# Splitting the last two down panels of every tile into two sweeps over output blocks

## The reference, cut to what matters

```python
gate = lora_add(jnp.einsum('bnh,fh->bnf', x, W_gate), x, A_gate, B_gate)
up   = lora_add(jnp.einsum('bnh,fh->bnf', x, W_up), x, A_up, B_up)
act  = jax.nn.silu(gate) * up
down = lora_add(jnp.einsum('bnf,hf->bnh', act, W_down), act, A_down, B_down)
return x + down
```

## Time and profile before

| | us |
|---|---|
| median of 3 runs | 2187.39 (2184.78 to 2189.65) |
| profiled execution | 2185.16 |
| its span in the trace | 2183.5 |

### The profile page before, as it was taken

The page is one execution under the profiler, slowest core; times in us unless marked ns, Lnnn a source line. Parts: engine busy times, 40 slices in busy tenths (PEclk is TensorE's granted clock), DMA queues, the critical chain, the costliest instruction groups (busy, mean ns, idle before and its releaser), DMA issues.

```text
span 2183.5 us, 34214 instructions
## 1 busy us (share of the span) xinstructions
PE 2087.3 (96%) x10432; PEld 1774.5 (81%) x10432; DVE 1610.3 (74%) x2144; ACT 971.2 (44%) x1282; POOL 99.0 (5%) x167
## 2 busy tenths in 40 slices
PE   2998999999996899999999999999999999999998
PEld 2997888888885788888888888888888888878887
DVE  7777999999997778787877337458787878753433
ACT  2222888788883533333433325343333333333232
POOL 3110000000001230000000000000000000000000
PEclk9999999999998999999999999999999999999999
DMA  5999999989986664333434995444343434264543
GB/s 194 376 364 347 351 349 356 356 331 349 351 345 235 188 199 129 93 110 89 110 92 147 252 259 187 173 120 118 91 110 94 108 96 108 70 217 159 183 154 125
DMA packets 254658, 441.49 MB, mean 202 GB/s; under 512 B 146902, under 2 KB 147094, under 8 KB 234390
## 3 DMA queue, kind: packets, MB, share of 16 engines
q1 hardware_dynamic: 241046, 408.69, 56.4%
q0 software_dynamic: 11392, 32.01, 4.4%
q10 hardware_dynamic: 2176, 0.26, 0.1%
HBM read 400.74 MB, written 63.73 MB: 213 GB/s over the span
## 4 chain that ended last, share of the span: by engine, by line
PE 82%; DVE 8%; DMA 4%; ACT 2%; issue 2%; DVEq 1%; POOL 0%; ACTq 0%; SPq 0%; POOLq 0%
PE ps L1849 19%; PE ps L1850 19%; PE ps L1851 19%; PE ps L1793 4%; PE ps L1795 4%; PE ps L1794 4%; PE ps L1769 4%; DMA W<-in_w 3%; PE ps L1894 2%; PE ps L1893 2%; DVE wl L1318 2%; PE ps L1802 1%; PE ps L1925 1%; PE ps L1926 1%; DMA araw<-picked_a 1%
## 5 line engine op out<-in xcount | busy, mean ns | idle before, releaser
L1849 PE MATMUL ps<-bh,oph 128*128 128x512 f32 x1216 | 476.3, 392 | 9.2 <-ACT tmp L807 6.0
L1850 PE MATMUL ps<-bl,oph 128*128 128x512 f32 x1216 | 475.8, 391 | 0.0
L1851 PE MATMUL ps<-bh,opl 128*128 128x512 f32 x1216 | 474.2, 390 | 0.0
L1318 DVE TENSOR_TENSOR wl<-W,wh 128x2048 fp32r<-128x2048 f32 x152 | 343.6, 2285 | 9.9 <-ACT wh L742 9.0
L1406 DVE TENSOR_TENSOR tmp<-ps,tmp 128x512 f32<-128x512 f32 (+1 forms) x340 | 234.1, 689 | 132.0 <-PE ps L1894 67.5
L742 ACT ACTIVATE wh<-W 128x2048 fp32r<-128x2048 f32 x152 | 290.7, 1915 | 61.0 <-DMA W<-in_w 55.1
L1403 DVE TENSOR_TENSOR wdl<-wraw,wdh 128x1024 fp32r<-128x1024 f32 x92 | 112.6, 1224 | 264.2 <-ACT wdh L807 264.2
L1849 PE MATMUL ps<-acb_h,wdh 128*128 128x512 f32 (+1 forms) x736 | 280.8, 382 | 4.8 <-DVE acb_l L1403 4.8
L1850 PE MATMUL ps<-acb_l,wdh 128*128 128x512 f32 (+1 forms) x736 | 279.8, 380 | 0.0
L1851 PE MATMUL ps<-acb_h,wdl 128*128 128x512 f32 (+1 forms) x736 | 279.7, 380 | 0.0
L1849 PEld LDWEIGHTS ps<-bh,oph 128*128 128x128 f32 x1216 | 229.4, 189 | 54.6 <-DVE opl L1403 10.4
(11 more groups left out here) (205 smaller groups left out, 2794.9 us busy)
## 6 DMA issues: line engine op xcount, KB each, us to landing
W<-in_w SPq DMA_DIRECT2D x152, 1024.0 KB, 6.9
raw<-in_wgu SPq DMA_DIRECT2D x168, 256.0 KB, 2.7
wraw<-in_wd SPq DMA_DIRECT2D x84, 512.0 KB
toep<-kpad SPq DMA_DIRECT2D x32, 1024.0 KB, 9.3
lraw<-picked_b SPq DMA_DIRECT2D x88, 256.0 KB, 3.8
raw<-kept_acts SPq DMA_DIRECT2D x88, 256.0 KB, 3.4
kept_acts<-tmp SPq DMA_DIRECT2D x84, 256.0 KB, 2.3
picked_b<-in_lora_b POOLq DMA_DIRECT2D x32, 352.0 KB, 4.9
```

The source lines that it names most:

```text
L1318: V.tensor_tensor(out=wl[:, c], in0=W[:, c], in1=wh[:, c].bitcast(F32), op=ALU.subtract).then_inc(w_lo, 1)
L1849: mm(to, lhsT=wh, rhs=mh, start=start, stop=False)
L1850: mm(to, lhsT=wh, rhs=ml, start=False, stop=False)
L1851: return mm(to, lhsT=wl, rhs=mh, start=False, stop=stop)
```

## The change

The loop over pairs of panels is one round shorter. Panel 20 of each tile is written out whole. Panels 21 and 22 are then run in two sweeps: blocks 0 to 3 of panel 21, blocks 0 to 3 of panel 22, blocks 4 to 7 of panel 21, blocks 4 to 7 of panel 22. `panel_done` is raised for panel 21 after its last block, thus at three quarters of the two panels' work, and for panel 22 at the end. Nothing else is edited; ACT, DVE, SP and GpSimd keep their programs.

```diff
+            def last_panels(tile):
+
+                end, a = (tile + 1) * NPAN, (FT - 1) % 2
+                pe.wait_ge(wd_lo, end - 2)
+                pe.wait_ge(ac_lo, (tile + 1) * FT - 2)
+                down(tile, end - 3, a, range(LT)).then_inc(panel_done, 1)
+                for outs in (range(LT // 2), range(LT // 2, LT)):
+                    pe.wait_ge(wd_lo, end - 1)
+                    pe.wait_ge(ac_lo, (tile + 1) * FT - 1)
+                    earlier = down(tile, end - 2, 1 - a, outs)
+                    pe.wait_ge(wd_lo, end)
+                    pe.wait_ge(ac_lo, (tile + 1) * FT)
+                    last = down(tile, end - 1, a, outs, stop=True)
+                    if LT - 1 in outs:
+                        earlier.then_inc(panel_done, 1)
+                        last.then_inc(panel_done, 1)
+
             def other_panels(tile):
...
-                with pe.Fori(0, (NPAN - HALF_AT - 3) // 2) as i:
+                pairs = (NPAN - HALF_AT - 3) // 2
+                with pe.Fori(0, pairs - 1) as i:
                     panel_pair(tile, HALF_AT + 2, i)
-                pe.wait_ge(wd_lo, (tile + 1) * NPAN)
-                pe.wait_ge(ac_lo, (tile + 1) * FT)
-                down(tile, tile * NPAN + NPAN - 1, (FT - 1) % 2, range(LT), stop=True).then_inc(panel_done, 1)
+                last_panels(tile)
```

## The result

The changed kernel took 2195.82 us (median of 8 runs, 2193.18 to 2203.22) against 2186.09 for the kernel before (8 runs beside it, 2183.8 to 2189.65): ratio 1.0041, 95% interval 1.0027 to 1.0055. It is slower by 0.4%, as forecast (2195.0). Its profiled execution took 2194.26, span 2192.6, which is 9.1 us above the span of before; the sum had said 7.6. The two medians lie 9.7 apart, and the interval of the ratio spans 5.9 to 12.0 us, so the timed runs show that there is a loss but don't fix its size; the traces do.

What follows compares the result with a forecast made beforehand. PE, busy 96% of the span, was taken to bound the kernel. Terms 4.88 (starts of tiles 1 and 3) + 2.64 (stage 1) + 0.62 - 0.5 (tile 3) = +7.6 us gave 2195.0, range 2190.5 to 2199.5.

Steps and rivals of the forecast that it cites:

- Gate 1: End of each tile's first sweep: PE waits for panel 22's low parts, wanted after half a panel; 0.62 us per tile.
- Gates 1 to 3: Starts of tiles 1 and 3: waits before panel 22, for the first add, before panel 1; 0.62 + 1.33 + 0.49 = 2.44 us.
- Gate 4: Tile 1 to stage 1: PE waits for an add, 0.92 us, then for `apl`, 1.10; with gate 1, 2.64.
- Tail: End of tile 3: the first store goes out earlier, so the second no longer queues behind it; -0.5 us.
- Sum: Whole kernel, all waits less the gain at the end: +7.6 us, 0.35%.
- Late loads: Rival, tiles 1 and 3: panel 3's loads run beside the stores and come late; +9.6 us, 2197.0; 12%.
- Early adds: Rival, tile ends: adds run early and panel 21's late report costs nothing; +2.0 us, 2189.4; 7%.
- the chain fits: Rival, panel 22's copy: ACT and DVE ready within 2.72 us, so only the store's head start remains; -0.5, 2186.9; 7%.
- The clock rival: New idle gaps halve PE's clock: 5.4 us more per panel, +18 at two starts, 2206; 2%.
- My gaps are at most 1.3: Argument against a clock fall: PE's new idle gaps stay within 1.3 us, while a window with 2 us idle kept full clock.
- gate 2: Starts of tiles 1 and 3: PE waits for DVE's first add, queued behind the late `panel_lo(0)`; 1.33 us with restart.

Runs made afterwards that it cites:

- short_chain: The changed kernel with panel 22's weights copied and subtracted in two halves, so PE's first sweep over it waits for the first half only; ratio 1.0028.
- late_report: The kernel before, whole panels without sweeps, with only panel 21's report moved to the first matmul of block 4 of panel 22; ratio 1.0041.
- dve_order: The changed kernel with adds 0 to 3 put ahead of the next low parts in DVE's order at tile ends; ratio 1.0024.
- control: The kernel before, unchanged, profiled a second time; ratio 1.0001.
- split53: The changed kernel with sweeps of five and three blocks instead of four and four, in all tiles; ratio 1.0032.
- tile3_split53: The kernel before with sweeps of five and three blocks in tile 3 alone, tiles 0 to 2 as before; ratio 1.0003.

## Why the prediction was right

- **Gate 1**, 0.62 a tile: measured 0.70 (tile 3 to the last matmul, 11.09 against 10.39). PE went on 0.15 us after `acb_l`'s end (1306.24 + 0.68 to 1307.07), where the earlier trace rows had 0.06. short_chain shows the mechanism.
- **Gates 1 to 3** at the starts of tiles 1 and 3, 2.44 each: measured 2.67 and 2.61. Late_report and dve_order show the two causes, report and order. By the starts of successive matmuls, 0.227 apart where nothing waits, the three gates at the start of tile 1 took 0.69, 1.41 and 0.43, against 0.62, 1.33 and 0.49 in the sum; the 0.1 that is left over is spread thin and not explained.
- **Gate 4** with gate 1, 2.64: measured 2.63 against control. The memsets came 24.20 us after tile 1's anchor instead of 19.44, thus 4.8 later and not about 3, and stayed hidden: the copy at 1455.50 still waited 7.71 for PE.
- **Tail**, -0.5: measured -0.6, with landings of 5.0 and 5.0. All ten profiles agree: where the second store is issued 2.7 us behind the first (before, control, late_report) they take 5.1 and 5.6, where it is 4.8 to 5.4 behind, 5.0 and 5.0. The estimate of 4.4 us by the Trainium skill, DMA: Bandwidth & Descriptors, section "Anatomy of one DMA", was reached in none of them, and the gain of 1.2 by it did not come.
- **Sum**, 7.6: measured 8.0 from anchor to anchor. The 9.1 between the two spans is 8.0, plus 1.6 for the clock at stage 1's start, less 0.5 from the work before the first anchor (1304.53 to 1304.01). That the median came out 0.8 from the forecast is partly luck: the forecast stood on a median of before of 2187.39 from three runs, and the eight beside the changed kernel gave 2186.09; the loss itself was 9.7 by medians and 8.0 by distances, for 7.6.
- **Rivals.** Late loads did not bite: in the changed kernel the weight copies for panel 3 (1328.39 and 2075.18) waited for PE and not for a transfer. Early adds did not happen: `acb_l` ended at 1315.79 and the adds began at 1315.82; dve_order made them early, and 3.5 us of loss stayed. That the chain fits came true only when it was made shorter. The clock rival was priced at a whole panel per start, 5.4; when it did happen, in split53, it cost 1.2. The argument from "My gaps are at most 1.3" held for the changed kernel, whose own gaps caused no fall, but I had missed that the kernel's own wait of 2.5 us at stage 1's start usually brings one. I had also written that the trace of before shows a fall only at the idle end, and that is wrong: it has others before the down products, one of them around a wait of PE of 3.47 that ended at 731.47, where the clock is 0.50 over 6.83 us.

```profile
731.47 0.77 PE L1849 MATMUL ps<-bh,oph 128*128 128x512 f32 x1 [3.47 <-ACT tmp L807]
```
```profile
730.04:736.87 6.83, 5.41 (x13) 4.28 (x14) 5.72 (x9) 2.61 (x5) 2.31 (x4) 0.50 0.85 248
```

- A reading that only the experiments gave: the terms of a start are not independent. split53 removed gate 1 and lost it again at gate 2.

## What to carry to other kernels

When a buffer slot is given back by a report of progress, reordering the work inside that buffer's lifetime moves the report, and every preparation behind it; look first at the distance from the report to the next need (here 5.44 us of cover for a chain of 3.24) and ask what the new order leaves of it. Early results help only if the engine that takes them is not bound by a fixed order to something that became later. Compare small changes from anchor to anchor inside the traces: timed runs of the kernel before went from 2182.2 to 2195.7 us here, for an effect of 8.

## What the runs showed of the hardware

From the down product of tile 0 on, the granted clock fell to its lower level after quite short waits of PE. It did so behind the wait of 2.5 us at stage 1's start in nine of ten profiles, for about 3.4 us of the clock's record, at a cost of 1.6 us; once behind a wait of 1.85 us (split53, tile 1), at a cost of 1.2; and once behind one of 2.70 (tile3_split53, at 1233.70, before the first anchor, so in no distance of the table). The same wait of 2.5 us left it at 1.00 in the first profile of the kernel before, the same wait of 1.85 did so at the start of tile 3 in split53, and so did one of 2.11 in control (1226.52) and one of 1.80 or 1.81 in tile 0 of every profile. So the length of the wait alone did not decide, in these runs, whether it fell; what else does stays open.

The second of two stores of 1 MB from GpSimd took 5.6 us to land when it was issued 2.7 us behind the first, and 5.0 when it was issued 4.8 to 5.4 us behind it.
